# A gated delta-rule decoder layer on one core: the output tile in two buffers, its block transpose placed later on VectorE, and the key-key copy as one VectorE product

## The chip, the cores and the metric

The kernel runs on one core of a Trainium2 chip. A core has five instruction streams that run side by side and meet only at semaphores: TensorE (PE, matmuls, with its weight loads shown apart as PEld), VectorE (DVE), ScalarE (ACT), GpSimd (POOL) and SyncE (SP), which here only issues DMAs. Each stream executes its instructions in program order; one that waits holds back all behind it. The metric is the device time of the whole kernel in microseconds, lower is better.

## The reference

One decoder layer in float32: a gated delta-rule attention block, a cross-attention block, and a feed-forward block with ternarized weights. The change lies in the first of them, for 4 sequences of 512 tokens, 16 key heads and 32 value heads of 128 columns. Cut to what matters:

```python
mixed = silu(causal_conv1d(hidden @ w_qkv, conv_w))
q, k, v = split(mixed)
q, k = l2norm(q), l2norm(k)
def step(St, inp):
    St = St * exp(g_t)
    v_old = k_t @ St
    delta = (v_t - v_old) * b_t
    St = St + outer(k_t, delta)
    o = q_t @ St
    return St, o
core = scan(step)
core = core * rsqrt(mean(core * core) + EPS) * norm_weight
core = core * silu(z)
return core.reshape(...) @ w_out
```

The kernel does not step through tokens. It takes 128 tokens at a time (a chunk, 4 of them in a sequence), builds the 128x128 matrix of key-key products of a chunk, inverts a triangular matrix made of it in six levels, and carries the state from chunk to chunk.

## The kernel before

`delta_rule` works through 64 units, one for each pair of key head (16) and sequence (4). A unit holds one key head, its two value heads and all four chunks. Four stages of four neighbouring units are interleaved in a **slot**: `project` (unit n: projections, convolution, key norm, key-key products), `invert` (unit m = n-1: levels 0 to 4 of the inversion), `recur` (unit s = n-2: level 5, refinement, and the recurrence over the chunks) and `finish` (unit f = n-3: the last chunks, normalisation, gate, store of the output). There are 67 slots; all but the first three and the last three have all four stages. The order inside a slot is written by hand in a `slot` function for each engine, so nothing but these lists and the semaphores sets the order.

The parts that the prediction follows, by line:

- The output tile `oo` (L343) holds the two heads' four chunks of one unit. `first_output` (L1270, ScalarE) writes chunk 0, `output` (L1087, VectorE) chunks 1 to 3. ScalarE squares them (`o_square`, L1275), GpSimd makes the norm (`o_norm`), ScalarE scales (`o_scale`, L1232), GpSimd gates (`o_gate`, L691), VectorE turns blocks of 32x32 into `ob` (`flip_o`, L1046), and SP stores `ob` with 16 DMAs of 32 KB (`store_o`, L580). With one `oo`, `first_output` of the next unit waits until `flip_o` has read it (L1272).
- In VectorE's slot `flip_o(f)` stands between `level_z(m, 2)` and `residual(s, 1, 0)` (L1148). TensorE's `solve(s, 1)` (L881) waits for both residuals of chunk 1.
- The key-key products of unit n (`kk`, L782, TensorE) leave PSUM by `copy_kk` (L1225, ScalarE): four 128x128 copies, each scaled by a chunk's key norm, into `kks`. Behind it on ScalarE stands `copy_d(m, 3)` (L1246), for which TensorE's `level_z(m, 4)` (L807) waits. GpSimd's `b_full` (L659) reads `kks`.
- The key norm: VectorE turns k into `kf` (`flip_k`, L1041), SP writes it out with 4 DMAs (`store_k`, L553), waits until they have landed and loads it back as `kn` (`load_k`, L560). ScalarE's `k_square` (L1203) waits for `kn`. Behind it on ScalarE stand `copy_kq(m)` (L1242), `first_output(s)` and `copy_d(m, 2)`.
- SP's list for a slot (L491 to L520): weights of the next group if it is time (three places), `move_q` of unit s (16 DMAs of 16 KB, L572), another weight load, `load_decay` for unit n+1, `store_k(n)`, `load_k(n)`, `store_v(m)`, weights, `load_v(m)`, `store_o(f)`, a weight load. Weights change every fourth slot; their six tiles and the taps are loaded one by one, each when its last reader is done.

Of the kernel before, what the change touches and what calls it, by code (L numbers as in the profile page):

```python
# [6 lines left out]
P = 128  # L7
F32 = mybir.dt.float32
F16 = mybir.dt.float16
BF16 = mybir.dt.bfloat16  # L10
# [72 lines left out]
def at(n, per, k):  # L83

    q, r = n
    return q * (ROUND * per) + (r * per + k)
# [6 lines left out]
def back(n, d):  # L93
    return n[0], n[1] - d


def wait(eng, sem, value):

    if not isinstance(value, int) or value > 0:
        eng.wait_ge(sem, value)  # L100


def chunk(ap, c):
    return ap[:, c * P:(c + 1) * P]
# [215 lines left out]
def delta_rule(nc, xT, tabs, cons, nw, wc, w_loaded, taps_loaded, acc, early_loaded, early_weighed, decay_dram, w_dram, k_dram, v_dram, core_dram, wout):  # L320

    with ExitStack() as ctx:
# [17 lines left out]
        tt = [many(f"tt{i}_", GV, [P, S]) for i in range(2)]  # L340
        state, rr, uu, oq = sb("state", [P, GV * P]), sb("rr", [P, GV * P]), sb("uu", [P, GV * P]), sb("oq", [P, GV * P])
        vb, ob = sb("vb", [P, NC, GV * NC, 32]), sb("ob", [P, NC, GV * NC, 32])
        oo = sb("oo", [P, GV, NC, P])  # L343
        junk, kqs, kks = sb("junk", [P, 3 * NC, P], BF16), sb("kqs", [P, S]), sb("kks", [P, S])
        kss, qss, rkt, rk = sb("kss", [P, NC]), sb("qss", [P, NC]), sb("rkt", [P, NC]), many("rk", 2, [P, 2, NC])
        qf, qn = sb("qf", [P, NC, NC, 32]), sb("qn", [P, NC, NC, 32])
        eq = many("eq", 4, [P, NC])
# [33 lines left out]
        def count(n, before=0):  # L381

            return at(back(n, before), 1, 1)
# [48 lines left out]
        def per_token(ap):  # L432
# [6 lines left out]
        RING_BANK = {"q": 1, "k": 2, "z1": 0, "v1": 1, "z0": 0, "kq": 2, "v0": 0, "kk": 1}  # L439
        RING_FREED = {"k": (taps, "taps", 2), "q": (taps, "taps", 5), "v0": (taps, "taps", 8), "v1": (taps, "taps", 11),  # L440
                      "z0": (z_silued, "z_silued", 0), "z1": (z_silued, "z_silued", 1),
                      "kk": (kk_copied, "squares", NC - 1), "kq": (kqs_ready, "squares", NC - 1)}
        CONV_ORDER = ("k", "v1", "v0", "q")
        CONV_BUFFER = {name: i % 2 for i, name in enumerate(CONV_ORDER)}
        SILUED = {"k": (silued, "silued", 0), "q": (silued, "silued", 1), "v0": (silued, "silued", 2), "v1": (silued, "silued", 3)}
# [150 lines left out]
        def _(pool):  # L596
# [56 lines left out]
                nc.gpsimd.tensor_tensor(eq[n[1] % 4][:, :], qss[:, :], cons[:, C_RMS:C_RMS + NC], ALU.add).then_inc(eq_ready, 1)  # L653

            def b_full(n, h):
                pool.wait_ge(kk_copied, at(n, NC, NC))
                pool.wait_ge(gams_ready, nth(n, "gams_ready", h))
                wait(pool, bl_ready, nth(n, "bl_ready", h, 1))
                nc.gpsimd.tensor_tensor(bf[h][:, :], kks[:, :], gam[h][:, :], ALU.mult).then_inc(bf_ready, 1)  # L659
# [29 lines left out]
                                        ALU.pow).then_inc(or_ready, 1)  # L689

            def o_gate(s, h):  # L691
                o = oo[:, h, :, :]
                pool.wait_ge(o_scaled, at(s, GV * NC, h * NC + NC))
                pool.wait_ge(z_silued, at(s, GV, GV))
                nc.gpsimd.tensor_tensor(o, o, sz[s[1] % 2][:, :, h * P:(h + 1) * P], ALU.mult).then_inc(gated, 1)  # L695
# [313 lines left out]
        def _(dve):  # L1009
# [30 lines left out]

            def flip_k(n):  # L1041
                dve.wait_ge(silued, nth(n, "silued", 0))
                wait(dve, k_moved, at(back(n, 1), 80, 64))
                nc.vector.transpose(kf[:, :, :, :], kT[third(n)][:, :].rearrange("p (c b j) -> p b c j", c=NC, b=NC)).then_inc(k_flipped, 1)

            def flip_o(s):  # L1046
                dve.wait_ge(gated, at(s, GV, GV))
                wait(dve, stored, at(back(s, 1), STORES, STORES))
                nc.vector.transpose(ob[:, :, :, :], oo[:, :, :, :].rearrange("p h c (a j) -> p a (h c) j", a=NC)).then_inc(o_flipped, 1)

            def flip_e0(m):
                dve.wait_ge(e0_ready, at(m, 2 * GV, 2 * GV))
# [28 lines left out]
            def next_state(s, c, h):  # L1081
# [2 lines left out]
                nc.vector.scalar_tensor_tensor(chunk(state, h), chunk(state, h), tab(s, Q_CDEC, h, c),  # L1084
                                               chunk(psa, h), ALU.mult, ALU.add).then_inc(s_ready, 1)

            def output(s, c):  # L1087
                dve.wait_ge(o_done, at(s, NC, c + 1))
                dve.wait_ge(oq_ready, at(s, 6, 2 * c))
                nc.vector.tensor_tensor(oo[:, :, c, :], psb[:, 0:GV * P].rearrange("p (h d) -> p h d", h=GV),  # L1090
                                        oq[:, :].rearrange("p (h d) -> p h d", h=GV), ALU.add).then_inc(o_ready, 1)

            def slot(n, project, invert, recur, finish):
                m, s, f = back(n, 1), back(n, 2), back(n, 3)
                if project:
                    decays(n, 1)
                if invert:
                    convolve(m, 1, 1)
                    convolve(m, 1, 2)
                    convolve(m, 1, 3)  # L1100
                if recur:
                    level_z(s, 5)
                if finish:
                    next_state(f, 2, 0)
                if project:
                    convolve(n, 0, 1)
                if finish:
                    next_state(f, 2, 1)
                if project:
                    convolve(n, 0, 2)  # L1110
                    decays(n, 0)
                if finish:
                    output(f, 2)
                    residual(f, 3, 0)
                if project:
                    convolve(n, 0, 3)
                if recur:
                    refine(s, 0)
                if finish:
                    residual(f, 3, 1)  # L1120
                if recur:
                    refine(s, 1)
                if project:
                    flip_k(n)
                if invert:
                    flip_e0(m)
                if recur:
                    close(s, 1)
                    close(s, 0)
                if invert:  # L1130
                    level_z(m, 0)
                if project:
                    convolve(n, 3, 1)
                if finish:
                    output(f, 3)
                if invert:
                    flip_v(m)
                    flip_d(m, 0)
                    level_z(m, 1)
                if project:  # L1140
                    convolve(n, 3, 2)
                if project:
                    convolve(n, 3, 3)
                if invert:
                    flip_d(m, 1)
                    level_z(m, 2)
                if finish:
                    flip_o(f)  # L1148
                if recur:
                    residual(s, 1, 0)  # L1150
                    residual(s, 1, 1)
                if invert:
                    flip_d(m, 2)
                    level_z(m, 3)
                if recur:
                    next_state(s, 1, 0)
                    next_state(s, 1, 1)
                if recur:
                    residual(s, 2, 1)
                    residual(s, 2, 0)  # L1160
                    output(s, 1)
                if invert:
                    level_z(m, 4)
                    flip_d(m, 3)
                if project:
                    convolve(n, 2, 1)
                    convolve(n, 2, 2)
                    convolve(n, 2, 3)
                if invert:
                    flip_q(m)  # L1170
# [4 lines left out]
        def _(act):  # L1175
# [27 lines left out]
            def k_square(n):  # L1203
                act.wait_ge(k_moved, at(n, 80, 80))
                wait(act, rk_ready, at(back(n, 1), 3, 1))
                wait(act, k_squares, at(back(n, 1), NC, NC))
                squares(lambda c: kn[n[1] % 2][:, :, c, :], lambda c: junk[:, c, :].rearrange("p (a j) -> p a j", j=32), kss, k_squares)

            def q_square(n):
                act.wait_ge(q_moved, at(n, MOVED, MOVED))  # L1210
# [11 lines left out]
                wait(act, refined, nth(n, "refined", h, 2))  # L1222
                nc.scalar.activation(bh[n[1] % 2][h][:, :], bf[h][:, :], ACT.Copy).then_inc(bh_ready, 1)

            def copy_kk(n):  # L1225
                act.wait_ge(kk_done, count(n))
                act.wait_ge(rk_ready, at(n, 3, 2))
                wait(act, bf_ready, at(back(n, 1), GV, GV))
                for c in range(NC):
                    nc.scalar.activation(chunk(kks, c), chunk(bank("kk"), c), ACT.Copy, scale=rk[n[1] % 2][:, 0, c:c + 1]).then_inc(kk_copied, 1)  # L1230

            def o_scale(s, h):  # L1232
                act.wait_ge(or_ready, at(s, 2, 2))
                for c in range(NC):
                    o = oo[:, h, c, :]
                    nc.scalar.activation(o, o, ACT.Copy, scale=r2[:, h, c:c + 1]).then_inc(o_scaled, 1)  # L1236

            def copy_kq(m):
# [30 lines left out]

            def first_output(s):  # L1270
                act.wait_ge(o_done, at(s, NC, 1))
                wait(act, o_flipped, count(s, 1))  # L1272
                nc.scalar.activation(oo[:, :, 0, :], psb[:, 0:GV * P].rearrange("p (h d) -> p h d", h=GV), ACT.Copy).then_inc(first_ready, 1)

            def o_square(s, c, h):  # L1275
                if c == 0:
                    act.wait_ge(first_ready, at(s, 2, 2))
                    wait(act, or_ready, at(back(s, 1), 2, 1))
                else:
                    act.wait_ge(o_ready, at(s, NC - 1, c))  # L1280
                nc.scalar.activation(junk[:, NC + h * NC + c, :], oo[:, h, c, :], ACT.Square, scale=HD ** -0.5,
                                     accum_out=oss[:, h, c:c + 1]).then_inc(o_squares, 1)

            def slot(n, project, invert, recur, finish):
# [52 lines left out]
                if recur:  # L1337
                    solved(s, 1)
                    read_q(s, 1, 1)
                    read_q(s, 1, 0)  # L1340
                if project:
                    copy_kk(n)
                if invert:
                    copy_d(m, 3)
                if project:
# [794 lines left out]
```

## Time and profile before

| | us |
|---|---|
| median of 3 runs | 3383.51 (3382.04 to 3384.68) |
| the profiled execution | 3382.74 |
| its span | 3380.9 |
| TensorE busy | 3202.4 (95%) |
| VectorE busy | 2222.3 (66%) |
| GpSimd busy | 1946.0 (58%) |
| ScalarE busy | 1794.1 (53%) |

The loop of slots takes about three quarters of the span, from some 80 us to some 2500 us; what follows is cross-attention and feed-forward, in which VectorE, ScalarE and GpSimd are mostly idle and which the change does not touch. The granted TensorE clock is 1.00 through the loop (the higher of its two levels, 2.4 GHz). A slot repeats in steps of 37.65 us to within a few hundredths, so one slot read closely stands for the loop. In the timelines an idle time in brackets is the engine's own wait just before the instruction, with what ended it. The SP queue issues DMAs and is not counted as an engine; a merged row of its timeline (x16) runs from the first issue to the end of the last, waits between them included.

### The profile page before, as it was taken

What the parts mean: (1) busy time and instruction counts of PE and PEld (TensorE: products, weight loads), DVE (VectorE), ACT (ScalarE), POOL (GpSimd) and SP (SyncE); (2) the same over time, 40 slices, a digit from 0 to 9 for tenths busy, and PEclk for the clock granted to TensorE, in tenths of its full rate; (3) what the DMA queues carried; (4) which work ended last, traced back from release to release, by engine and by line L of the source; (5) the groups of instructions that cost most, each with busy time, mean ns of one, the idle gap of its engine ahead of it and who ended that gap; (6) DMA issues with size and microseconds to landing.
All of it is one profiled execution on the core that took longest, in us unless ns stands there. A gap on an engine that the chain in (4) does not pass through costs nothing. (4 is left out here: it accounts for less than half of the span.)

```text
span 3380.9 us, 59978 instructions
## 1 busy us (share of the span) xinstructions
PE 3202.4 (95%) x20064; PEld 2087.9 (62%) x20064; DVE 2222.3 (66%) x3366; ACT 1794.1 (53%) x5623; POOL 1946.0 (58%) x1888
## 2 busy tenths in 40 slices
PE   5899999999999999999999999999988999999999
PEld 2567666766676667666766666666663444454444
DVE  6788888878888888888888887888840100024553
ACT  2466666666666666666666666666652000011232
POOL 2677777777777777777777777777740000011132
PEclk8999999999999999999999999999989999999999
DMA  3233333333333333333343333333325222211001
GB/s 100 58 91 92 92 85 86 92 87 86 80 101 89 86 84 95 90 80 85 91 98 87 80 90 93 89 80 92 101 70 196 75 100 87 99 38 63 0 13 38
DMA packets 469200, 282.30 MB, mean 83 GB/s; under 512 B 311808, under 2 KB 410240, under 8 KB 463360
## 3 DMA queue, kind: packets, MB, share of 16 engines
q1 hardware_dynamic: 467600, 271.39, 30.2%
q10 hardware_dynamic: 1296, 7.09, 0.5%
q8 instruction: 163, 2.67, 0.3%
q14 instruction: 141, 1.16, 0.1%
HBM read 173.17 MB, written 88.34 MB: 77 GB/s over the span
## 5 line engine op out<-in xcount | busy, mean ns | idle before, releaser
L762 PE MATMUL acc<-xT,wc 128*128 128x512 f32 x2048 | 937.0, 601 | 9.4 <-ACT d_kks L1230 7.4
L762 PEld LDWEIGHTS acc<-xT,wc 128*128 128x128 f32 x2048 | 370.8, 191 | 381.2 <-issue 380.7
L1019 DVE SCALAR_TENSOR_TENSOR d_conv<-acc,wc,d_conv 128x511 f32<-128x511 f32 (+2 forms) x768 | 566.2, 737 | 36.6 <-ACT d_conv L1182 25.2
L775 PE MATMUL acc<-wc,xT 128*128 128x256 f32 x2048 | 473.4, 384 | 0.0
L775 PEld LDWEIGHTS acc<-wc,xT 128*128 128x128 f32 x2048 | 379.1, 190 | 46.3
L1064 DVE CAST_PREDICATED d_zm<-cons,d_tz 128x512 f16<-128x512 int32 x384 | 265.4, 691 | 160.3 <-PE d_tz L807 153.6
L1057 DVE STREAM_TRANSPOSE d_em<-d_dm 128x1024 f16<-128x1024 f16 x256 | 314.8, 1230 | 40.8 <-ACT d_dm L1246 40.8
L1542 PE MATMUL acc<-t_area 128*128 128x512 f32 x768 | 332.5, 592 | 0.8 <-ACT t_area L1991 0.8
L2048 POOL TENSOR_SCALAR t_veps<-t_mv 128x1 f32<-128x1 f32 x32 | 9.7, 303 | 546.1 <-DVE t_mv L1787 546.1
L1246 ACT ACTIVATE d_dm<-acc 128x512 f16<-128x512 f32 x384 | 229.8, 598 | 121.8 <-PE acc L820 121.8
L1182 ACT ACTIVATE d_conv<-acc,wc 128x512 f32<-128x512 f32 x256 | 177.2, 692 | 219.8 <-PE acc L762 172.0
L695 POOL TENSOR_TENSOR d_oo<-d_oo,d_sz 128x512 f32<-128x512 f32 x128 | 160.0, 1271 | 196.3 <-ACT d_oo L1236 196.3
L1777 DVE TENSOR_TENSOR t_x<-acc,t_x 128x512 f32<-128x512 f32 x16 | 11.1, 691 | 392.3 <-PE acc L1542 392.3
L1542 PEld LDWEIGHTS acc<-t_area 128*128 128x128 f32 x768 | 144.6, 190 | 177.2 <-issue 176.9
L659 POOL TENSOR_TENSOR d_bf<-d_kks,d_gam 128x512 f32<-128x512 f32 x128 | 160.1, 1271 | 154.0 <-ACT d_kks L1230 153.9
L665 POOL TENSOR_TENSOR d_pT<-d_kqs,d_gamc 128x512 f32<-128x512 f32 x128 | 217.3, 1719 | 0.0
L1939 ACT ACTIVATE xT<-t_turn 128x512 f32<-128x512 f32 x32 | 18.2, 596 | 369.7 <-PE t_turn L1524 369.7
L807 PEld LDWEIGHTS d_tz<-d_dm,d_bh 128*128 128x128 f16 x3072 | 137.9, 98 | 117.2 <-ACT d_dm L1246 47.5
L807 PE MATMUL d_tz<-d_dm,d_bh 128*128 128x64 f16 x3072 | 154.5, 193 | 40.1 <-ACT d_dm L1246 35.0
L1028 DVE TENSOR_TENSOR_SCAN d_gam<-d_decay,d_ident 128x512 f32<-128x512 f32 x128 | 190.9, 1491 | 0.9 <-DMA d_decay<-decay_rows 0.8
L643 POOL TENSOR_TENSOR d_em<-d_bh,cons 128x512 f16<-128x512 f16 x128 | 190.7, 1490 | 0.0
L881 PE MATMUL d_psa<-d_rr,d_tt 128*128 128x128 f32 x768 | 128.3, 290 | 56.2 <-DVE d_rr L1078 56.2
(224 smaller groups left out, 6979.2 us busy)
## 6 DMA issues: line engine op xcount, KB each, us to landing
d_decay<-decay_rows SPq DMA_DIRECT2D x64, 512.0 KB, 5.1
v_rows<-d_vb SPq DMA_DIRECT2D x256, 128.0 KB, 2.6
d_vn<-v_rows SPq DMA_DIRECT2D x64, 512.0 KB, 3.7
core_rows<-d_ob SPq DMA_DIRECT2D x1024, 32.0 KB, 1.7
t_area<-core_rows SPq DMA_DIRECT2D x30, 1024.0 KB, 4.8
wc<-in_w SPq DMA_DIRECT2D x96, 256.0 KB, 3.1
k_rows<-d_kf SPq DMA_DIRECT2D x256, 64.0 KB, 3.2
d_kn<-k_rows SPq DMA_DIRECT2D x64, 256.0 KB, 2.9
```

The source lines that it names most:

```text
L643: nc.gpsimd.tensor_tensor(by_chunk(half(em[i2], h)), by_chunk(bh[i2][h]), bc(cons[:, C_B2T:C_B2T + P], NC), ALU.mult).then_inc(e0_ready, 1)
L665: nc.gpsimd.tensor_tensor(pT[m[1] % 2][h][:, :], kqs[:, :], gamc[m[1] % 2][h][:, :], ALU.mult).then_inc(p_ready, 1)
L762: last = nc.tensor.matmul(bank(TILE[j])[:, :], wtile(j, k), xT[:, k, r % B * S:(r % B + 1) * S], start=k == 0, stop=k == KT - 1)
L775: last = nc.tensor.matmul(bank(f"z{j}")[:, i * GV * P:(i + 1) * GV * P].rearrange("p (h n) -> p h n", h=GV), xT[:, k, r % B * S + (2 * j + ...
L807: last = nc.tensor.matmul(packed(tz, l, (h * NC + c) * HALF, HALF), chunk(bh[m[1] % 2][h], c), even(dm, l, (h * NC + c) * P, P), start=Tru ...
L1019: nc.vector.scalar_tensor_tensor(c[:, d:S], bank(TILE[j])[:, 0:S - d], tap(j, KS - 1 - d), c[:, d:S], ALU.mult, ALU.add).then_inc(taps, 1)
L1028: nc.vector.tensor_tensor_scan(gam[h][:, :], decay[:, h, :], ident[:, :], 0.0, ALU.mult, ALU.add).then_inc(gam_ready, 1)
L1057: nc.vector.transpose(em[m[1] % 2][:, :], dm[:, :]).then_inc(flipped, 1)
L1064: nc.vector.copy_predicated(even(zm[l], l), bc(mask, GV * NC), packed(tz, l)).then_inc(z_ready, 1)
L1182: nc.scalar.activation(conv_of(TILE[j])[:, :], bank(TILE[j])[:, :], ACT.Copy, scale=tap(j, KS - 1)).then_inc(tap0, 1)
L1246: nc.scalar.activation(even(dm, l), packed(td, l), ACT.Copy).then_inc(d_copied, 1)
L1542: return nc.tensor.matmul(acc[t][:, :], core_of(grp, t, q, h), rhs, start=head == 0, stop=head == HV - 1)
```

## The change

- `oo` is two buffers, taken in turn by the unit's number. `first_output(s)` now waits for `flip_o` of two units before, not one.
- `flip_o(f)` moves down VectorE's list, from behind `level_z(m, 2)` to behind `level_z(m, 4)` and `flip_d(m, 3)`, just ahead of the three `convolve(n, 2, ...)`.
- `copy_kk(n)` leaves ScalarE and becomes one VectorE product of the whole PSUM bank with the key norms broadcast over each chunk. It stands behind the two `next_state(s, 1, ...)` and ahead of `residual(s, 2, ...)`.
- To pay for the second buffer, the scratch tile `junk` shrinks: the squares of k are written into `kf` and six of the eight squares of the output into `ob`. For that `flip_k` waits for the squares of the unit before, and six `o_square` and `flip_o` get one more wait each.
- SP's list is as it was.

```diff
-        oo = sb("oo", [P, GV, NC, P])
-        junk, kqs, kks = sb("junk", [P, 3 * NC, P], BF16), sb("kqs", [P, S]), sb("kks", [P, S])
+        oo = many("oo", 2, [P, GV, NC, P])
+        junk, kqs, kks = sb("junk", [P, GV, P], BF16), sb("kqs", [P, S]), sb("kks", [P, S])
...
             def flip_k(n):
-                wait(dve, k_moved, at(back(n, 1), 80, 64))
+                wait(dve, k_squares, at(back(n, 1), NC, NC))
...
             def flip_o(s):
                 dve.wait_ge(gated, at(s, GV, GV))
                 wait(dve, stored, at(back(s, 1), STORES, STORES))
-                nc.vector.transpose(ob[:, :, :, :], oo[:, :, :, :].rearrange("p h c (a j) -> p a (h c) j", a=NC)).then_inc(o_flipped, 1)
+                dve.wait_ge(o_squares, at(s, GV * NC, GV * NC))
+                nc.vector.transpose(ob[:, :, :, :], oo[s[1] % 2][:, :, :, :].rearrange("p h c (a j) -> p a (h c) j", a=NC)).then_inc(o_flipped, 1)
...
+            def copy_kk(n):
+                dve.wait_ge(kk_done, count(n))
+                dve.wait_ge(rk_ready, at(n, 3, 2))
+                wait(dve, bf_ready, at(back(n, 1), GV, GV))
+                nc.vector.tensor_tensor(by_chunk(kks), by_chunk(bank("kk")), per_token(rk[n[1] % 2][:, 0, :]), ALU.mult).then_inc(kk_copied, 1)
...
-                if finish:
-                    flip_o(f)
                 if recur:
                     residual(s, 1, 0)
                     residual(s, 1, 1)
...
                     next_state(s, 1, 0)
                     next_state(s, 1, 1)
+                if project:
+                    copy_kk(n)
                 if recur:
                     residual(s, 2, 1)
                     residual(s, 2, 0)
...
                     level_z(m, 4)
                     flip_d(m, 3)
+                if finish:
+                    flip_o(f)
...
-                squares(lambda c: kn[n[1] % 2][:, :, c, :], lambda c: junk[:, c, :].rearrange("p (a j) -> p a j", j=32), kss, k_squares)
+                squares(lambda c: kn[n[1] % 2][:, :, c, :], lambda c: kf[:, :, c, :], kss, k_squares)
...
-            def copy_kk(n):
-                act.wait_ge(kk_done, count(n))
-                act.wait_ge(rk_ready, at(n, 3, 2))
-                wait(act, bf_ready, at(back(n, 1), GV, GV))
-                for c in range(NC):
-                    nc.scalar.activation(chunk(kks, c), chunk(bank("kk"), c), ACT.Copy, scale=rk[n[1] % 2][:, 0, c:c + 1]).then_inc(kk_copied, 1)
...
             def first_output(s):
                 act.wait_ge(o_done, at(s, NC, 1))
-                wait(act, o_flipped, count(s, 1))
+                wait(act, o_flipped, count(s, 2))
...
-                nc.scalar.activation(junk[:, NC + h * NC + c, :], oo[:, h, c, :], ACT.Square, scale=HD ** -0.5,
+                if (c, h) in ((1, 0), (0, 1)):
+                    out = junk[:, h, :]
+                else:
+                    wait(act, stored, at(back(s, 1), STORES, STORES))
+                    out = ob[:, c, h * NC:(h + 1) * NC, :].rearrange("p b j -> p (b j)")
+                nc.scalar.activation(out, oo[s[1] % 2][:, h, c, :], ACT.Square, scale=HD ** -0.5,
...
-                if project:
-                    copy_kk(n)
                 if invert:
                     copy_d(m, 3)
```

VectorE in the middle of a slot, before (`d_ob<-d_oo` is `flip_o`, `d_rr` the residuals, `d_em<-d_dm` `flip_d`, `d_zm` `level_z`, `d_state` `next_state`):

```order
L1049 STREAM_TRANSPOSE d_ob<-d_oo 128x1024
L1078 SCALAR_TENSOR_TENSOR d_rr<-d_psa,d_tabm,d_vn 128x128 x2
L1057 STREAM_TRANSPOSE d_em<-d_dm 128x1024
L1064 COPY_PREDICATED d_zm<-cons,d_tz 128x32x16
L1084 SCALAR_TENSOR_TENSOR d_state<-d_state,d_tabm,d_psa 128x128 x2
L1078 SCALAR_TENSOR_TENSOR d_rr<-d_psa,d_tabm,d_vn 128x128 x2
L1090 TENSOR_TENSOR d_oo<-d_psb,d_oq 128x2x128
L1064 COPY_PREDICATED d_zm<-cons,d_tz 128x16x32
L1057 STREAM_TRANSPOSE d_em<-d_dm 128x1024
L1019 SCALAR_TENSOR_TENSOR d_conv<-acc,wc,d_conv 128x511
```

The same place on VectorE now:

```order
L1079 SCALAR_TENSOR_TENSOR d_rr<-d_psa,d_tabm,d_vn 128x128 x2
L1058 STREAM_TRANSPOSE d_em<-d_dm 128x1024
L1065 COPY_PREDICATED d_zm<-cons,d_tz 128x32x16
L1085 SCALAR_TENSOR_TENSOR d_state<-d_state,d_tabm,d_psa 128x128 x2
L1092 TENSOR_TENSOR d_kks<-acc,d_rk 128x512
L1079 SCALAR_TENSOR_TENSOR d_rr<-d_psa,d_tabm,d_vn 128x128 x2
L1097 TENSOR_TENSOR d_oo<-d_psb,d_oq 128x2x128
L1065 COPY_PREDICATED d_zm<-cons,d_tz 128x16x32
L1058 STREAM_TRANSPOSE d_em<-d_dm 128x1024
L1050 STREAM_TRANSPOSE d_ob<-d_oo 128x1024
L1019 SCALAR_TENSOR_TENSOR d_conv<-acc,wc,d_conv 128x511
```

The transpose into `ob` moved from ahead of ten instructions to behind them, and the product into `kks` is new among them.

ScalarE from `first_output` to the next convolution tap, before (`d_dm<-acc` is `copy_d`, `d_uu` `solved`, `d_oq` `read_q`):

```order
L1242 ACTIVATE d_kqs<-acc,d_rk 128x128 x4
L1273 ACTIVATE d_oo<-d_psb 128x2x128
L1246 ACTIVATE d_dm<-acc 128x64x8
L1264 ACTIVATE d_uu<-d_psa 128x256
L1255 ACTIVATE d_oq<-d_psb,d_tabm 128x128 x2
L1230 ACTIVATE d_kks<-acc,d_rk 128x128 x4
L1246 ACTIVATE d_dm<-acc 128x32x16
L1182 ACTIVATE d_conv<-acc,wc 128x512
```

And now:

```order
L1248 ACTIVATE d_dm<-acc 128x64x8
L1266 ACTIVATE d_uu<-d_psa 128x256
L1257 ACTIVATE d_oq<-d_psb,d_tabm 128x128 x2
L1248 ACTIVATE d_dm<-acc 128x32x16
L1191 ACTIVATE d_conv<-acc,wc 128x512
```

The four copies ahead of the second `copy_d` are gone.

## Rows read from the trace of the kernel before

**Rows 1.** Waits from 400 to 2400 us: total us, times, longest us.
```profile
PE d_psa L881 <- DVE d_rr L1078: 43.1, 53, 0.8
PE d_tz L807 <- ACT d_dm L1246: 27.4, 52, 0.5
```
**Rows 2.** Timeline of one slot, ScalarE: start, duration, instruction, idle before.
```profile
1016.42 0.30 ACT L1201 ACTIVATE d_junk<-d_kn 128x128 bf16<-128x128 f32 x1
...
1019.30 0.38 ACT L1273 ACTIVATE d_oo<-d_psb 128x256 f32<-128x256 f32 x1 [0.60 <-DVE d_ob L1049]
1019.58 0.59 ACT L1246 ACTIVATE d_dm<-acc 128x512 f16<-128x512 f32 x1
...
1022.59 1.14 ACT L1230 ACTIVATE d_kks<-acc,d_rk 128x128 f32<-128x128 f32 x4 [1.03 <-PE acc L782]
```
**Rows 3.** Timeline of the same slot, VectorE.
```profile
1017.96 1.25 DVE L1049 STREAM_TRANSPOSE d_ob<-d_oo 128x1024 f32<-128x1024 f32 x1 [1.74 <-POOL d_oo L695]
...
1020.20 1.25 DVE L1057 STREAM_TRANSPOSE d_em<-d_dm 128x1024 f16<-128x1024 f16 x1 [0.51 <-ACT d_dm L1246]
...
1023.33 0.61 DVE L1078 SCALAR_TENSOR_TENSOR d_rr<-d_psa,d_tabm,d_vn 128x128 f32<-128x128 f32 x2 [0.80 <-PE d_psa L860]
...
1024.71 0.69 DVE L1064 CAST_PREDICATED d_zm<-cons,d_tz 128x512 f16<-128x512 int32 x1 [0.44 <-PE d_tz L807]
...
1026.48 2.27 DVE L1019 SCALAR_TENSOR_TENSOR d_conv<-acc,wc,d_conv 128x511 f32<-128x511 f32 x3
```
**Rows 4.** Groups by line and form, 400 to 2400 us: busy us, mean ns.
```profile
L1028 DVE TENSOR_TENSOR_SCAN d_gam<-d_decay,d_ident 128x512 f32<-128x512 f32 x106 | 158.4, 1495 | 0.0
...
L1069 DVE TENSOR_TENSOR d_zr<-d_imd,d_tz 128x512 f16<-128x512 f16 x53 | 36.4, 688 | 1.8 <-issue 0.3 <-POOL d_imd L678 0.3
```
**Rows 5.** Timeline of the SP queue, a slot without weight loads ahead of `load_k`.
```profile
1019.23 8.05 SPq L586 DMA_DIRECT2D core_rows<-d_ob  x16
1029.40 10.02 SPq L577 DMA_DIRECT2D d_qn<-d_qf  x16
1039.78 0.39 SPq L487 DMA_DIRECT2D d_decay<-decay_rows  x1
1041.92 1.84 SPq L557 DMA_DIRECT2D k_rows<-d_kf  x4
1045.73 0.34 SPq L563 DMA_DIRECT2D d_kn<-k_rows  x1
```
**Rows 6.** Timeline of the SP queue, first and last slot with three weight loads.
```profile
642.12 7.78 SPq L586 DMA_DIRECT2D core_rows<-d_ob  x16
649.95 6.39 SPq L481 DMA_DIRECT2D wc<-in_w  x3
656.74 10.02 SPq L577 DMA_DIRECT2D d_qn<-d_qf  x16
...
667.48 1.85 SPq L557 DMA_DIRECT2D k_rows<-d_kf  x4
672.38 0.34 SPq L563 DMA_DIRECT2D d_kn<-k_rows  x1
...
2315.01 10.53 SPq L577 DMA_DIRECT2D d_qn<-d_qf  x16
...
2331.55 0.34 SPq L563 DMA_DIRECT2D d_kn<-k_rows  x1
```
**Rows 7.** Timeline of the SP queue, a slot with a weight load behind `move_q`.
```profile
2277.79 10.95 SPq L577 DMA_DIRECT2D d_qn<-d_qf  x16
...
2295.01 0.34 SPq L563 DMA_DIRECT2D d_kn<-k_rows  x1
```
**Rows 8.** Line L586's DMA issues, 400 to 2400 us: ns min/median/max.
```profile
L586 SPq DMA_DIRECT2D core_rows<-d_ob x848: 302/451/1968, 415.5 to 2383.5; - x170
```
**Rows 9.** Timelines of the SP queue and of ScalarE, a slot whose `kn` came late.
```profile
1391.03 0.34 SPq L563 DMA_DIRECT2D d_kn<-k_rows  x1
...
1393.92 0.31 ACT L1201 ACTIVATE d_junk<-d_kn 128x128 bf16<-128x128 f32 x1 [0.61 <-DMA d_kn<-k_rows]
```

More of the change, by code:

```diff
@@ L441, in delta_rule @@
                       "z0": (z_silued, "z_silued", 0), "z1": (z_silued, "z_silued", 1),
-                      "kk": (kk_copied, "squares", NC - 1), "kq": (kqs_ready, "squares", NC - 1)}
+                      "kk": (kk_copied, "once", 0), "kq": (kqs_ready, "squares", NC - 1)}
         CONV_ORDER = ("k", "v1", "v0", "q")
@@ L655, in b_full @@
             def b_full(n, h):
-                pool.wait_ge(kk_copied, at(n, NC, NC))
+                pool.wait_ge(kk_copied, count(n))
                 pool.wait_ge(gams_ready, nth(n, "gams_ready", h))
@@ L691, in o_gate @@
             def o_gate(s, h):
-                o = oo[:, h, :, :]
+                o = oo[s[1] % 2][:, h, :, :]
                 pool.wait_ge(o_scaled, at(s, GV * NC, h * NC + NC))
@@ L1089, in output @@
                 dve.wait_ge(oq_ready, at(s, 6, 2 * c))
-                nc.vector.tensor_tensor(oo[:, :, c, :], psb[:, 0:GV * P].rearrange("p (h d) -> p h d", h=GV),
+                nc.vector.tensor_tensor(oo[s[1] % 2][:, :, c, :], psb[:, 0:GV * P].rearrange("p (h d) -> p h d", h=GV),
                                         oq[:, :].rearrange("p (h d) -> p h d", h=GV), ALU.add).then_inc(o_ready, 1)
@@ L1234, in o_scale @@
                 for c in range(NC):
-                    o = oo[:, h, c, :]
+                    o = oo[s[1] % 2][:, h, c, :]
                     nc.scalar.activation(o, o, ACT.Copy, scale=r2[:, h, c:c + 1]).then_inc(o_scaled, 1)
@@ L1271, in first_output @@
                 act.wait_ge(o_done, at(s, NC, 1))
-                wait(act, o_flipped, count(s, 1))
-                nc.scalar.activation(oo[:, :, 0, :], psb[:, 0:GV * P].rearrange("p (h d) -> p h d", h=GV), ACT.Copy).then_inc(first_ready, 1)
+                wait(act, o_flipped, count(s, 2))
+                nc.scalar.activation(oo[s[1] % 2][:, :, 0, :], psb[:, 0:GV * P].rearrange("p (h d) -> p h d", h=GV), ACT.Copy).then_inc(first_ready, 1)
             def o_square(s, c, h):
```

## The prediction

> **What bounds the kernel now.** I read four views in this order. The first is the engine table: TensorE is busy for 95% of the span, so only what makes TensorE wait can be won. The second is the list of waits inside the loop, which names just two such waits, each once in a slot: 43.1 us in 53 slots, 0.81 each, for VectorE's residuals, and 27.4 us in 52, 0.53 each, for ScalarE's `copy_d` [rows 1]. The 53 slots fill 2000 us; from 642.12 to 1019.23 the store of the output comes up ten times [rows 5, 6], which gives 37.7 us for a slot, 150.8 for the four between one set of weights and the next. The third view is the timeline of VectorE and ScalarE around these waits, which shows their causes: `flip_o` stands idle for 1.74 us until GpSimd has gated the tile, runs for 1.25, and only then come the residuals [rows 3]; and the four `kk` copies, 1.14 us, stand ahead of `copy_d` [rows 2]. The fourth is the timeline of the SP queue. It is not an engine, nothing there is counted as busy and few wait for it, but it issues 43 DMAs in a slot in a fixed order, and `flip_o` starts a chain through it [rows 5].
>
> **The change part by part.** Times below are in the slot of [rows 2, 3] unless said otherwise.
>
> *The residual wait.* With `flip_o` out of the way the residuals run right behind `level_z(m, 2)`; VectorE was idle there. The 0.81 us goes. Next late is the state of chunk 1. It hangs on `copy_d(m, 2)`, which starts at 1019.58 because `first_output` ahead of it waited 0.60 for `flip_o` [rows 2]. With two buffers that wait goes too, and the chain `copy_d`, `flip_d`, `level_z`, `next_state` moves forward by 0.60 and no more, so TensorE gains 0.60 of the 0.81 there.
>
> *The `kk` copy.* ScalarE loses 1.14 us ahead of `copy_d(m, 3)`, more than the 0.53 that TensorE waits, so all of the 0.53 goes. VectorE gains one product. Its form is not in the trace. Its nearest row is a product-like instruction of the same 512 columns with one operand in PSUM, 0.69 us [rows 4]; the upper end is the slowest VectorE instruction of 512 columns, the scan, 1.49 [rows 4]; below it could not cost less than nothing. I take 0.69. What hides it is the 0.80 us in which VectorE waits for `read_k` ahead of `residual(s, 2)` [rows 3]; if it took 1.49, 0.7 would come out on the far side, 45 us over 64 slots.
>
> *Together on TensorE.* 0.60 + 0.53 = 1.13 us, which would make a slot 36.5 us, if nothing else became late.
>
> *`flip_o` and what is queued behind it on VectorE.* `flip_o` ends at 1017.96 + 1.25 = 1019.21 before. Where does it end now, counted from the start of `k_square` at 1016.42? `copy_d(m, 2)` ended at 1020.17, 0.60 of which is the wait that goes: 3.15 us behind `k_square` [rows 2]. From `flip_d` at 1020.20 to the convolution at 1026.48 are 6.28 us, less the 0.44 that `level_z(m, 4)` waited for the late `copy_d` [rows 3]: 5.84. The 0.80 in it is taken by the product and stays. Then comes `flip_o`, 1.25. Neighbours overlap a little, so 10.2 us in all, where it was 1019.21 - 1016.42 = 2.8. The transpose is 7.4 us later in the slot. On VectorE that costs nothing: the three convolutions behind it start where they did (all ahead of them comes earlier by about as much as the transpose takes), and their readers have microseconds to spare.
>
> *The SP queue.* Every DMA of `store_o` now starts 7.4 us later, and so does what SP issues behind it in its list: `move_q`, `load_decay`, `store_k`, `load_k`. Nobody is in a hurry for the stores or for q. But ScalarE's `k_square` waits for `kn`, and behind it stand `copy_kq`, `first_output` and `copy_d(m, 2)`, for which TensorE waits. Before, SP had slack in a slot without weights: it stood idle from 1027.28 to 1029.40 for `flip_q` and from 1040.17 to 1041.92 for `flip_k`, and `kn`, issued at 1045.73, landed some 5 us ahead of `k_square` at 1054.07, one slot behind 1016.42 [rows 2, 5]. 7.4 us is more than that together. So the queue closes a loop, `flip_o` to `store_o` to `kn` to `k_square` to `flip_o`, and its length is the sum:
>
> - `store_o`: 16 issues of 0.451 us (median) and 0.05 between them, 8.0 [rows 8]; 8.05 and 7.78 in the slots shown [rows 5, 6]. I take 8.1.
> - from the start of `move_q` to the issue of `load_k`, with nothing between that SP waits for but landings. The slots with three weight loads ahead of `move_q` show it, since SP is already late there: 15.64 in the first, 16.54 in the last [rows 6], 12 such slots in all, 15.6 to 17.8 with a mean of 16.8. It is 10 for `move_q`, 2.5 for `load_decay` and `store_k`, 3 to 5 for the landing.
> - from the issue of `load_k` to the start of `k_square`, when that waits: 1391.03 to 1393.92, 2.9 [rows 9].
> - `k_square` to the end of `flip_o`: 10.2, from above.
>
> The sum is 8.1 + 16.8 + 2.9 + 10.2, with 0.05 between issues, 38.05: longer than TensorE's 36.5, and longer than the 37.7 of before. In every fourth slot a weight load stands ahead of `move_q` and one behind it: 17.22 from `move_q` to `load_k` in the slot shown [rows 7], mean 17.1 of 12, and 0.45 more for the load ahead: 38.85. In the next slot three stand ahead of `move_q`. The 6.39 us of [rows 6] are mostly a wait for their tiles' readers; 7.4 us later they are free, and three issues are 1.35: 39.4. Four slots are 2 x 38.05 + 38.85 + 39.4 = 154.35, against 150.8 before: 3.55 us slower.
>
> That a late `kn` holds up the whole slot is seen in the trace as it is: in the slot of [rows 9] ScalarE waited 0.61 for it, and that slot was 37.9 us long where its neighbours had 37.7.
>
> *A page's rule.* Row first: 16 small stores keep the SP queue busy for 8 us, though each lands within 2 us or so [rows 8]. The Trainium skill, DMA: Bandwidth & Descriptors, section "Rules for kernel authors", says for overlap: issue the DMA early, compute, and wait for it late, and its fixed cost overlaps. The change makes an issue late that nobody waits for soon, so by a reading that counts only landings it is free, which is the first rival; by the rows the issues themselves are what is paid, since another transfer stands behind them.
>
> *The new waits.* `flip_k` waits for `k_squares` of the unit before, 24 us old by then. The six `o_square` that write into `ob` wait for its stores; these are issued by 8.1 us behind `flip_o` and land 2 later, and the first such square comes about 12 behind `flip_o`: hidden, by 2 us. `flip_o` waits for squares that the scaling needed anyway. Nothing for these.
>
> *The sum.* 15 sets of four slots run this loop: +53 us. The last set has no weights to load: -2. The handful of slots at either end of the loop, where no `load_k` follows a `store_o`, gain TensorE's 1.13: -4. So +47 us on the profiled execution's 3382.7, which lies 0.8 under the median shown: 3430.
>
> **The rivals.**
>
> 1. *The queue keeps up.* If the loop through SP is under 36.5 us, TensorE sets the pace: 64 x 1.13 = 72 us off, 3311. For it: the parts at their shortest (7.8, 15.6, 2.9, 10.2) make 36.5, just TensorE's pace. Against it: this holds only without weights, and I have seen these minima singly, never together.
> 2. *The queue binds, but at its short values.* With every term at its shortest, the slots with weights take 37.2 and 37.9 and the others 36.5: 148.1 for four, 2.7 less than before, 3336. Halfway to my sum lies 3383, no change. Against it: the mean of 16.8 comes from 12 slots that were back to back as they would be now.
> 3. *The queue binds at its long values*, with 8.6 for the stores and 17.8 from `move_q` to `load_k`: 1.5 more in each of 60 slots, 3520; half of that is 3475. For it: SP has no idle time left in which a slow burst of issues (up to 1.97 us for one, [rows 8]) is caught up.
> 4. *The product on VectorE costs 1.49 us* and does not fit its hole. Since it lies on the same loop this adds up to 0.7 a slot, 45 us: 3475. Against it: nothing in its form asks for two passes.
>
> The other sign from my forecast is rivals 1 and 2; the point from which they decide is the loop of SP, at 37.7 us on average over four slots, 0.9 below my sum.
>
> **How the numbers follow.** A measurement of this kernel tells about 0.2%, 7 us, from no change. The queue binds and the kernel is slower by more than that: 0.74 (in it 0.06 for rivals 3 and 4 beyond 3475). It binds at short values: 0.05 for no change, 0.09 for faster. The queue keeps up: 0.12. The forecast is 3430. The range from 3345 to 3475 leaves out rival 1 with 0.12, a little of rival 2 and the long tail, 0.2 in all.
>
> **What the profile of the changed kernel would show.** If I am right: the SP queue's timeline has `store_o` and `move_q` back to back, with no gap; ScalarE's `k_square` waits for the DMA `d_kn<-k_rows` in nearly every slot, one to three us; TensorE waits ahead of `read_q` or `level_z(m, 3)`, for `first_output` or `copy_d`, where it had no wait; the waits of 0.81 and 0.53 are gone; ScalarE's wait for `flip_o` is gone; slots are 38 us, and 39 or more when weights change. If `k_square` does not wait, the loop is shorter than I think and rival 1 holds. If VectorE's residuals of chunk 2 wait for nothing and come late, the product is too dear. I would be wrong too if SP's issues got cheaper when back to back, or if `kf` landed sooner.

## The result: 3.7% slower

| | before | after |
|---|---|---|
| median | 3384.10 us (4 runs) | 3508.61 us (3507.43 to 3516.45, 4 runs) |
| ratio | | 1.0373, 95% interval 1.0355 to 1.0391 |
| span of the profiled execution | 3380.9 us | 3505.6 us |
| TensorE busy | 3202.4 us | 3257.1 us |
| mean granted TensorE clock | 0.990 | 0.973 |

The forecast was slower, 3430 us; the kernel came out 78 us beyond that and above the range. The direction and the place were right, the size was not: about 47 us were expected and 125 measured.

The waits inside the loop, after the change (columns as in [rows 1]):

```profile
ACT d_conv L1191 <- DMA wc<-in_w: 100.9, 12, 9.2
...
ACT d_kf L1210 <- DMA d_kn<-k_rows: 80.2, 38, 4.1
...
PE d_psb L868 <- ACT d_oo L1275: 71.3, 37, 3.9
...
PE d_psb L900 <- ACT d_oq L1257: 51.3, 12, 5.0
```

Both waits of [rows 1] are gone from TensorE's list. In their place stand two that were not there: `read_q(s, 1)` (L868) waits for `first_output`, 1.9 us in 37 slots, and `attend(f, 2)` (L900) waits for ScalarE's `read_q`, 4.3 us in 12 slots. Behind the first is `k_square` (L1210), late for `kn`; that is the forecast's mechanism. Behind the second is the first convolution tap (L1191), late for the taps, a load of 8 KB out of `wc`; the forecast had no such wait.

The SP queue from one weight change to the next, after the change:

```profile
1036.91 9.06 SPq L586 DMA_DIRECT2D core_rows<-d_ob  x16
1046.07 10.01 SPq L577 DMA_DIRECT2D d_qn<-d_qf  x16
...
1056.81 1.86 SPq L557 DMA_DIRECT2D k_rows<-d_kf  x4
1063.12 0.34 SPq L563 DMA_DIRECT2D d_kn<-k_rows  x1
...
1075.97 8.63 SPq L586 DMA_DIRECT2D core_rows<-d_ob  x16
...
1101.09 0.34 SPq L563 DMA_DIRECT2D d_kn<-k_rows  x1
...
1114.11 8.64 SPq L586 DMA_DIRECT2D core_rows<-d_ob  x16
...
1155.20 7.70 SPq L586 DMA_DIRECT2D core_rows<-d_ob  x16
1162.94 1.40 SPq L481 DMA_DIRECT2D wc<-in_w  x3
```

`store_o` and `move_q` stand back to back, without the 2 us of [rows 5] between them. From store to store the slots take 39.1, 38.1 and 41.1 us, and the next store comes at 1198.01, 42.8 later. From 400 to 2400 us the means from store to store are 38.1 us for the plain slots (26 of them, 36.6 to 41.0), 40.3 for those whose store is followed by one weight load ahead of `move_q` (13) and 43.1 for those with three loads (12). The forecast had 38.05, 38.85 and 39.4. A set of four slots so takes 5.3 us more than forecast: 3.7 of them in the slot with three loads, 1.5 in the one with one load. Over 15 sets that is 79 us, about the 78.

### The profile page after: what moved, and what is told of

Same layout as the page of the kernel before. It is cut to its first block and busy times, and to the rows that moved or that the text cites. A ratio compares the mean times of both kernels' runs of the same rounds, so it can differ in the third digit from the quotient of the medians.

```text
span 3505.6 us, 60101 instructions
## 1 busy us (share of the span) xinstructions
PE 3257.1 (93%) x20064; PEld 2132.3 (61%) x20064; DVE 2261.2 (65%) x3430; ACT 1730.9 (49%) x5367; POOL 1918.8 (55%) x1888
## 5 line engine op out<-in xcount | busy, mean ns | idle before, releaser
L1191 ACT ACTIVATE d_conv<-acc,wc 128x512 f32<-128x512 f32 x256 | 175.0, 684 | 304.5 <-PE acc L762 178.1
L678 POOL TENSOR_TENSOR d_imd<-cons,d_dm 128x512 f16<-128x512 f32 x128 | 210.5, 1645 | 126.4 <-ACT d_dm L1248 121.3
L900 PE MATMUL d_psb<-d_uu,d_pT 128*128 128x128 f32 x1024 | 172.0, 292 | 66.7 <-ACT d_oq L1257 66.7
L1028 DVE TENSOR_TENSOR_SCAN d_gam<-d_decay,d_ident 128x512 f32<-128x512 f32 x128 | 218.6, 1708 | 2.0 <-POOL d_bf L659 1.2
L868 PE MATMUL d_psb<-d_state,d_qT 128*128 128x256 f32 x384 | 120.0, 395 | 84.7 <-ACT d_oo L1275 84.7
L900 PEld LDWEIGHTS d_psb<-d_uu,d_pT 128*128 128x128 f32 x1024 | 145.0, 198 | 75.5 <-issue 66.8
```

What stands on the lines that cost most here:

```text
L678: nc.gpsimd.tensor_tensor(half_of(imd, 5)[:, :, 0, :], bc(cons[:, C_ID + (1 - side) * HALF:C_ID + (2 - side) * HALF], GV * NC), half_of(dm ...
L900: last = nc.tensor.matmul(chunk(psb, h), chunk(pT[s[1] % 2][h], c), chunk(uu, h), start=True, stop=True)
L1028: nc.vector.tensor_tensor_scan(gam[h][:, :], decay[:, h, :], ident[:, :], 0.0, ALU.mult, ALU.add).then_inc(gam_ready, 1)
L1191: nc.scalar.activation(conv_of(TILE[j])[:, :], bank(TILE[j])[:, :], ACT.Copy, scale=tap(j, KS - 1)).then_inc(tap0, 1)
```

## The experiments

All were compared with the kernel before on the same chip, which took 3383.5 to 3384.5 us each time, so that medians of different sessions can be set against each other. The edits are to the changed kernel, but for `kk_only` and `mid_single`, which start from the kernel before.

**`flip_mid`: the transpose two instructions behind its old place, ten ahead of the new one.**

```diff
                     residual(s, 1, 1)
+                if finish:
+                    flip_o(f)
                 if invert:
                     flip_d(m, 2)
...
                     flip_d(m, 3)
-                if finish:
-                    flip_o(f)
```

> The changed kernel with flip_o placed right behind the two residuals of chunk 1, instead of behind flip_d(m, 3). The transpose then runs at the same time in the slot as before the change (VectorE waits there for copy_d anyway), so everything behind store_o in the SP queue is as early as before. Theory (the loss of the change comes from the late stores, through the SP queue): k_square and the first tap wait for their DMAs no more than before, the two TensorE waits of 0.81 and 0.53 us are gone, 64 slots gain 1.1 to 1.2 us each: 3305 to 3315 us. Rival (the second buffer, the new waits or the product on VectorE cost the time): stays near 3500 us.

Measured: 3302.32 us, ratio to before 0.976 (0.9746 to 0.9775), 3 us below the range expected. VectorE in this kernel:

```profile
1027.77 1.25 DVE L1050 STREAM_TRANSPOSE d_ob<-d_oo 128x1024 f32<-128x1024 f32 x1 [1.23 <-POOL d_oo L695]
1029.41 1.25 DVE L1058 STREAM_TRANSPOSE d_em<-d_dm 128x1024 f16<-128x1024 f16 x1 [0.40 <-ACT d_dm L1248]
...
1031.66 0.68 DVE L1092 TENSOR_TENSOR d_kks<-acc,d_rk 128x512 f32<-128x512 f32 x1
1032.53 0.61 DVE L1079 SCALAR_TENSOR_TENSOR d_rr<-d_psa,d_tabm,d_vn 128x128 f32<-128x128 f32 x2 [0.19 <-PE d_psa L860]
```

The transpose fits between two waits of VectorE's own and delays nobody: the instruction behind it still waits 0.40 us for ScalarE. Everything else of the change is in this kernel, so all of the 206 us between it and the changed kernel come from where `flip_o` stands. The plain slots of this kernel take 36.34 us, in which TensorE hardly waits: that is its own pace. Those with weight loads ahead of `move_q` take 36.8.

**`flip_back`: the transpose at its old place.** The same edit, with `flip_o(f)` ahead of `residual(s, 1, 0)`.

> The changed kernel with flip_o at its old place ahead of the residuals; two output buffers and the product on VectorE stay. Theory: TensorE's wait for the residuals (0.81 us a slot) is back, its wait for copy_d(m, 3) (0.53) is gone, the SP queue is as before: 3384 - 64 x 0.53 = 3350 us. Rival (the product on VectorE or the shared scratch is what costs): above 3384 us.

Measured: 3345.22 us, 0.9883 (0.9867 to 0.99). TensorE waits 0.8 us in each slot for the residuals, as before, and not for `copy_d`:

```profile
PE d_psa L881 <- DVE d_rr L1079: 44.1, 54, 0.8
```

**`kk_only`: the product on VectorE, and nothing else, in the kernel before.** The product itself is that of the change; the waits on it follow.

```diff
                     next_state(s, 1, 1)
+                if project:
+                    copy_kk(n)
...
                     read_q(s, 1, 0)
-                if project:
-                    copy_kk(n)
```

> The kernel before with one part of the change: the product on VectorE in place of ScalarE's four copies. One output buffer, flip_o at its old place. Theory: it fits the hole ahead of residual(s, 2), TensorE's wait of 0.53 us for copy_d(m, 3) goes: 3384 - 34 = 3350 us. The rival of the prediction (the product takes up to 1.49 us and comes out behind its hole): 3384 us or more.

Measured: 3344.91 us, 0.9886 (0.9871 to 0.9901). The product alone brings 39 us, and with it the same time as `flip_back`: at the old place of `flip_o` the second buffer is worth nothing that shows.

**`mid_single`: one output buffer, with `flip_o` behind the residuals.** The kernel of `kk_only` with `flip_o(f)` moved behind `residual(s, 1, 1)`.

> The kernel before with the product on VectorE and flip_o behind the residuals of chunk 1, but with one output buffer. Theory: first_output waits for flip_o again and holds copy_d(m, 2) back by 0.6 us, from which the state of chunk 1 and TensorE's read_k(s, 2) hang: 64 x 0.6 = 38 us of what flip_mid gains is lost, 3335 to 3345 us. Rival (the second buffer buys nothing once the residuals come first): 3302 us.

Measured: 3341.01 us, 0.987 (0.9853 to 0.9886), 39 us more than with two buffers. TensorE no longer waits for the residuals, but the plain slots take 36.94 us, much as the 36.96 of `kk_only`. That is 0.6 us more than 36.34, as expected. What TensorE waits for now is `first_output`, 0.4 us a slot on average by its matmuls and 0.5 by the weight load ahead of them:

```profile
PE d_psb L868 <- ACT d_oo L1274: 20.4, 54, 0.8
```

So the second buffer and the place behind the residuals are worth 43 us together (`flip_mid` against `kk_only`), and singly nothing and 4 us, of which the 4 are within the noise (the intervals of `mid_single` and `kk_only` overlap).

**`q_late`: SP's order changed, the transpose left late.**

```diff
-                if recur:
-                    move_q(back(n, 2))
                 if project:
                     next_weights(n, 3)
...
                     load_k(n)
+                if recur:
+                    move_q(back(n, 2))
                 if invert:
                     store_v(back(n, 1))
```

> The changed kernel with one edit in SP's list: the 16 DMAs of move_q stand behind load_k instead of ahead of load_decay. Theory: load_k no longer queues behind 10 us of issues, so k_square waits for kn in no slot; three of four slots run at TensorE's 36.5 us. The slot after a weight load keeps its wait for the taps, which still stand behind store_o, and stays at 42 to 43 us. Four slots take 152 us instead of 160: 3385 to 3405 us. If kn were late for another reason than the queue of issues: 3500 us.

Measured: 3420.98 us, 1.0109 (1.0094 to 1.0124), 88 us less than the changed kernel, 16 more than the end of what was expected. `k_square` waits for `kn` nowhere in the loop, and the plain slots take 36.34 us, so the wait for `kn` was a matter of the issues ahead of it. The slots with three loads stay at 43.0 us. TensorE's wait there even grew:

```profile
1136.77 1.19 PE L900 MATMUL d_psb<-d_uu,d_pT 128*128 128x128 f32 x4 [5.70 <-ACT d_oq L1257]
```

What I had not counted are the slots ahead of these, 37.9 us on average: there SP waits for a tile's reader ahead of `store_k`, then issues `move_q` behind `load_k`, and reaches `store_o` late:

```profile
1092.88 7.57 SPq L481 DMA_DIRECT2D wc<-in_w  x2
...
1107.98 10.88 SPq L577 DMA_DIRECT2D d_qn<-d_qf  x16
...
1123.21 7.83 SPq L586 DMA_DIRECT2D core_rows<-d_ob  x16
```

**`taps_act`: the taps loaded from ScalarE's queue.**

```diff
-                if invert:
-                    next_weights(back(n, 1), TILES)
...
+                if j == 0 and r % B == 0 and not first(n):
+                    g = q * (ROUND // B) + r // B
+                    act.wait_ge(taps, at(back(n, 1), 12, 12))
+                    act.dma_start(wc[:, WCOLS:GCOLS], w_dram[g, :, WCOLS:GCOLS]).then_inc(taps_loaded, 16)
                 if j == 0 and r % B == 0:
```

> The changed kernel with the 16 small loads of the taps issued from ScalarE's queue, just ahead of the first tap that needs them, instead of from SP's. Theory of a second loop (flip_o, store_o, taps, first tap, read_q, attend): ScalarE's wait of 8 us for the taps falls to about 3, TensorE's wait of 4 us ahead of attend(f, 2) goes, and every fourth slot falls from 42.9 to the 39.4 us that the loop through kn gives: 15 x 3.5 = 52 us less, 3455 to 3465 us. Rival (only the loop through kn holds the time): 3500 to 3510 us.

Measured: 3448.96 us, 1.0189 (1.0168 to 1.0209), 60 us less than the changed kernel and 6 below the range expected. Of the wait for the taps this is left from 400 to 2300 us, 4.4 us a slot where it was 8.4:

```profile
ACT d_conv L1193 <- DMA wc<-in_w: 53.0, 12, 4.8
```

The slots that had three loads on SP, and now have two, come down from 43.1 to 39.1 us; 0.5 of the 4 us is the issue that SP no longer makes. So there is a second loop through the same queue: `flip_o`, the 8 us of `store_o`, the weight loads, the taps, the first tap.

**`q_late_taps_act`: both edits.**

> The changed kernel with both edits: move_q behind load_k on SP, and the taps loaded from ScalarE's queue; flip_o stays at its late place. Theory (the two loops through the SP queue are all of the loss): neither binds, three slots of four take TensorE's 36.3 us, the one in which SP is held by a weight load and stores late about 38: 3320 to 3345 us, faster than the kernel before. If the late transpose cost something on VectorE itself: above 3384 us.

Measured: 3323.06 us, 0.982 (0.9805 to 0.9835). With both loops opened the late transpose costs 21 us against `flip_mid`, and the kernel is faster than the one before. The plain slots take 36.34 us, as in `flip_mid`, so VectorE itself had room for the transpose; the 21 us lie in the slots with weight loads, 37.3 where `flip_mid` has 36.8, and at the ends of the loop.

**`filler` and `filler_half`: what does the low clock cost?** In the changed kernel the granted clock drops behind the long stalls. TensorE in stretches of 3 us; columns are the stretch, its length, PE's busy time, the granted clock, the DMA share and GB/s:

```profile
1303.00:1306.00 3.00, 1.42 (x14) 1.00 0.90 239
1306.00:1309.00 3.00, 1.33 (x9) 0.66 0.42 96
1309.00:1312.00 3.00, 3.00 (x22) 0.50 0.29 113
1312.00:1315.00 3.00, 3.00 (x25) 0.70 0.00 0
1315.00:1318.00 3.00, 3.00 (x10) 1.00 0.00 0
```

Ahead of it TensorE had stood still for 3.25 us; then it ran at 1.2 GHz (0.50), and from 1315 on again at 2.4. Behind a stall of 1.55 us in a plain slot the clock stayed at 1.00. The two stalls:

```profile
1307.67 1.19 PE L868 MATMUL d_psb<-d_state,d_qT 128*128 128x256 f32 x2 [3.25 <-ACT d_oo L1275]
...
1106.77 0.67 PE L868 MATMUL d_psb<-d_state,d_qT 128*128 128x256 f32 x2 [1.55 <-ACT d_oo L1275]
```

The Trainium skill, TensorE: Matmul & The Clock Gate, section "HAM oscillation — how this bites in real kernels", describes a kernel whose matmuls wait for a DMA in every step of a loop and start each next step at the low clock. By that page the stall is not all that is paid. The trace agrees for the stall of 3.25 us (0.50 behind it), and the experiment gives the price.

```diff
+            def filler(count):
+                for i in range(count):
+                    nc.tensor.matmul(tz[:, :], cons[:, 0:P], cons[:, 0:S], start=True, stop=True)
...
+                if finish and recur and invert and project and n[1] == 0:
+                    filler(4)
                 if finish:
                     attend(f, 2)
...
+                    if finish and invert and project and n[1] == 3:
+                        filler(3)
                     read_q(s, 1)
```

> The changed kernel with matmuls that compute nothing needed, placed on TensorE where it stands still longest: 8 of 128x512 float32 (0.44 us each, 3.5 us) ahead of attend(f, 2) in the slot that waits for the taps, and 7 (3.1 us) ahead of read_q(s, 1) in the slot before it. They write a PSUM bank that the next step of the inversion overwrites. The granted clock in the trace of the changed kernel falls to 1.2 GHz behind these two stalls, and the stretch from attend(f, 2) to level_z(m, 0) takes 9.1 us instead of 6.7, the one from read_q(s, 1) to the next projection 6.5 instead of 3.9. Theory (the low clock is a cost of its own, on top of the stalls): work put into the stalls keeps the clock at 2.4 GHz and the kernel gets faster although it does more: 15 x (2.4 + 2.4) = 70 us less, 3435 to 3460 us. Rival (the stall is all that is paid): 3508 us or a little more.

`filler` had 8 and 7 in place of 4 and 3. Measured: 3549.20 us, 1.0487 (1.0469 to 1.0506): slower, and above both expectations. That says nothing of the theory, since it put 7.1 and 6.2 us of work into stalls of 3.9 and 3.3.

> As the run filler, with half the filling: in that run's trace a float32 matmul of 512 columns stands as two rows, 0.88 us for both, so it put 7.1 and 6.2 us into stalls of 3.9 and 3.3 us. Here 4 matmuls (3.5 us) stand ahead of attend(f, 2) and 3 (2.7 us) ahead of read_q(s, 1). Theory (the low clock is a cost of its own): the clock stays at 2.4 GHz, the slots of 42.9 and 40.5 us become 40.3 and 39.0: 15 x 4.1 = 60 us less than the changed kernel, 3440 to 3460 us. Rival (the stall is all that is paid): 3508 us.

Measured: 3484.92 us, 1.0298 (1.0278 to 1.0317), 24 us less than the changed kernel though TensorE does some 90 us more work (15 sets of 3.5 and 2.7). That is neither the 60 us of the theory nor the nothing of its rival. The clock of the loop:

```profile
400.00:2400.00 2000.00, 1935.61 (x14011) 1.00 0.34 85
```

against this in the changed kernel:

```profile
400.00:2400.00 2000.00, 1871.25 (x13639) 0.97 0.34 83
```

So the low clock has a price of its own, and what could be won back of it is 24 us and not 60. The slots with one load came down by 0.5 us, to 39.8, and those with three by 1.2, to 41.95; 15 times the sum is 25. One reason why it was no more is seen in the slots with three loads of `filler_half`: with the clock up, TensorE comes to `refine` (L841) sooner and waits there for a `copy_d` that is late on ScalarE behind the first tap, 10.4 us in 12 slots where it was 2.2 in 4.

```profile
999.12 0.68 PE L900 MATMUL d_psb<-d_uu,d_pT 128*128 128x128 f32 x4 [1.14 <-ACT d_oq L1265]
...
1001.10 0.23 PE L841 MATMUL d_tz<-d_dm,d_bh 128*128 128x128 f16 x1 [0.86 <-ACT d_dm L1256]
```

**`mid_taps2_b`: `flip_mid` with the taps in two buffers.**

```diff
+                if project and n[1] == 1 and n[0] < G - 1:
+                    sp.wait_ge(taps, at(back(n, 1), 12, 12))
+                    sp.dma_start(tap_area(n[0] + 1), w_dram[n[0] + 1, :, WCOLS:GCOLS]).then_inc(taps_loaded, 16)
...
+        def tap_area(g):
+            return wc[:, WCOLS:GCOLS] if g % 2 == 0 else tapb[:, :]
+
+        def tap(n, j, k):
+            return tap_area((n[0] * ROUND + n[1]) // B)[:, j * KS + k:j * KS + k + 1]
```

> flip_o behind the residuals of chunk 1, and the taps in two buffers, the buffer chosen by the unit's group. Theory: the slots that wait for the taps come down from about 37.0 to 36.34 us: 3290 to 3299 us against 3302 with one buffer of taps. Rival (TensorE's work covers that wait): 3302 us.

Measured: 3294.99 us, 0.9738 (0.9723 to 0.9752), the lowest of all. An earlier form, `mid_taps2`, has the same instructions but took the taps of the wrong group for units at a group's border, and so computes something else; it ran in 3297.49 us, 0.9745 (0.973 to 0.9759), 1.5 us above the 3288 to 3296 expected of it. The gain over `flip_mid` is 5 to 7 us where 3 to 12 were expected of the second form; the intervals of the ratios overlap, so it is likely and not certain.

## Why the prediction was wrong in size, point by point

*TensorE's two waits.* Right: both went, and `flip_mid` shows their worth, 82 us against 72 forecast. The price of the first was mis-sized: 0.60 was taken, since the state of chunk 1 would be late next; TensorE's pace turned out as 36.34 us and not 36.5, so 1.3 us of a slot and not 1.13 were to be had.

*The product on VectorE.* Right. It measured 684 ns against 0.69 taken, and it left 0.19 us of the 0.80 of [rows 3]:

```profile
1108.88 0.59 DVE L1085 SCALAR_TENSOR_TENSOR d_state<-d_state,d_tabm,d_psa 128x128 f32<-128x128 f32 x2
1109.39 0.68 DVE L1092 TENSOR_TENSOR d_kks<-acc,d_rk 128x512 f32<-128x512 f32 x1
1110.27 0.61 DVE L1079 SCALAR_TENSOR_TENSOR d_rr<-d_psa,d_tabm,d_vn 128x128 f32<-128x128 f32 x2 [0.19 <-PE d_psa L860]
```

*The loop through `kn`.* Right in mechanism and size where it is alone: 38.05 forecast for a plain slot, 38.1 measured, and `q_late` takes the loop away and gets 36.34. It was no luck, since each term came out as taken. The terms of the sum, in us, means from 400 to 2400 us, read from the timelines of SP, ScalarE and VectorE:

| | stores and loads ahead of `move_q` | `move_q` to `load_k` | `load_k` to `k_square` | `k_square` to end of `flip_o` | slot |
|---|---|---|---|---|---|
| plain, forecast | 8.15 | 16.8 | 2.9 | 10.2 | 38.05 |
| plain, changed kernel | 8.36 | 16.69 | 2.92 | 10.12 | 38.1 |
| one load, forecast | 8.65 | 17.1 | 2.9 | 10.2 | 38.85 |
| one load, changed kernel | 8.84 | 17.44 | 3.04 | 10.97 | 40.3 |
| one load, `filler_half` | 9.53 | 17.37 | 2.88 | 10.03 | 39.8 |
| three loads, forecast | 9.5 | 16.8 | 2.9 | 10.2 | 39.4 |
| three loads, changed kernel | 9.92 | 16.31 | 6.77 | 10.12 | 43.1 |
| three loads, `filler_half` | 9.97 | 16.65 | 5.19 | 10.12 | 41.95 |
| the same slots, `taps_act` | 9.36 | 16.64 | 2.91 | 10.12 | 39.1 |

*"In the next slot three stand ahead of `move_q`: 39.4."* This is the step that failed. The slot takes 43.1, and the term that was mis-sized is the one from `load_k` to `k_square`: 6.8 us measured where 2.9 were taken. It is not `kn` that is late there: ScalarE's waits for it fall in the other slots, and ScalarE comes to `k_square` late. I had counted the three loads as 1.35 us of issue time ahead of `load_k`, as things in the way, and never asked who waits for them. One is the taps, for which ScalarE's first tap waits. In [rows 6] that wait could be read: the three loads span 6.39 us because the last of them is held for the old taps' readers, and it arrived last. The list behind [rows 1] had its waiter too, at the same filters and in the kernel before:

```profile
ACT d_conv L1182 <- DMA wc<-in_w: 41.3, 13, 3.3
```

I passed over it because TensorE did not wait there. ScalarE after the change:

```profile
1167.03 0.69 ACT L1191 ACTIVATE d_conv<-acc,wc 128x512 f32<-128x512 f32 x1 [8.02 <-DMA wc<-in_w]
```

and TensorE, for which ScalarE's `read_q` stands behind that tap:

```profile
1168.95 0.68 PE L900 MATMUL d_psb<-d_uu,d_pT 128*128 128x128 f32 x4 [3.89 <-ACT d_oq L1257]
```

This slot takes 42.8 us. In `taps_act` the term from `load_k` to `k_square` is back at 2.91 and the slot at 39.1, near the forecast; it recovers 60 us, most of the 78 by which the forecast was short.

*The clock.* No term of the sum had it: the forecast named waits of TensorE ahead of `read_q` and `level_z(m, 3)` and did not ask what the clock does behind them. `filler_half` puts 24 us on it, in the two kinds of slot with long stalls, and the table shows where: with three loads in the 6.77 that fall to 5.19, with one load in the 10.97 that fall to 10.03. In the slots with three loads it lies inside the late taps' price, so 60 and 24 are not to be added.

*The slot with one load: 38.85.* Mis-sized by 1.5 us, 22 us over 15 sets. 0.8 of it are in the stretch from `k_square` to the end of `flip_o`, which goes with the low clock, 0.3 in the stretch from `move_q` to `load_k`, and the rest in the stores and in small terms. With the clock up the slot still takes 39.8 us, because `store_o` itself took 8.9 us there instead of 8.25; why its 16 issues took longer stays open.

*The rivals.* The first, a queue that keeps up, is refuted by the 38 slots in which `k_square` waits for `kn`. The second, short values, is refuted by the terms of the plain slots, which came out at the means that the forecast took. The third had a time near the one measured, 3475 to 3520, by a wrong road: issues and landings in the plain slots were at their means, not at their long values. The fourth, a dear product, is refuted by its 0.68 us and by `kk_only`, which is faster than the kernel before.

*The ends of the range.* The upper end should have held the time and did not. It was made of spreads of terms that I had, and none was left for a reader of the queue that I had not looked for.

## What to carry to other kernels

When an instruction that feeds a DMA queue is moved, list everything that the queue issues behind it, and for each the engine that waits and how early it comes now, in the slots with extra transfers as well as in the plain ones; the taps missing from that list cost some 56 us here, where the whole forecast loss was 47. Before moving work far down an engine's list, look for one of the engine's own waits near the old place that it fits into: two instructions behind the old place gained 43 us against it, twelve behind (eleven of before and the product) lost 163. A long stall of TensorE may be paid twice, once as a stall and once at the low clock.

## What the runs showed of the hardware that was not expected

The granted clock fell to 1.2 GHz behind stalls of 3.25 and 3.89 us and held behind one of 1.55. Matmuls that are not needed, put into such stalls, kept it at 2.4 GHz (1.00 over the loop where it was 0.97) and made the kernel 24 us faster (ratio to before 1.0298 in place of 1.0373).

One DMA of `store_o` took the SP queue 0.45 us to issue (the median in [rows 8]), and 16 of them 7.7 to 9.3 us in the changed kernel, though no engine's wait in its loop ends with them. The 16 of `move_q` took 10.0 to 11.2 us; moving them behind `load_k` was worth 88 us.
